# Layer 0 of a two-layer graph network: another order for the first 34 pairs of edge tiles

## The reference, cut to what matters

```python
hid = silu(edge_scalars @ fc_w1 / 8);  w = hid @ fc_w2 / 8          # weights per edge, 224
es, ev = h_s[edge_src], h_v[edge_src]                               # (x @ lin1)[source]
m_s1 = w1 * es * e0;  m_s2 = w4 * dot(ev, e1) / 3
m_v1 = w2 * es * e1;  m_v2 = w3 * ev * e0;  m_v3 = w5 * cross(ev, e1) / 2
agg_s = segment_sum(concat(m_s1, m_s2), edge_dst);  agg_v = segment_sum(...)
o_s = agg_s @ lin2_ws;  o_v = agg_v @ lin2_wv                       # per node
x = layernorm(x + gated(sc + o))
```

## Time and profile before

| | |
|---|---|
| time, median of 3 runs | 2036.88 us (2024.79 to 2044.89) |
| the profiled execution, its own time | 2023.73 us |
| its span in the profile | 2022.0 us, 47808 instructions |
| busy over the span: PE, DVE, ACT, POOL | 1426.0, 1449.6, 1060.1, 1471.5 us |
| chain that ended last, shares | POOL 28%, issue 23%, DMA 16%, DVE 12%, PE 9%, ACT 8% |
| TensorE clock granted, mean | 0.88 |

### The profile page before, as it was taken

The page is one execution under the profiler, slowest core; times in us unless marked ns, Lnnn a source line. Parts: engine busy times, 40 slices in busy tenths (PEclk is TensorE's granted clock), DMA queues, the critical chain, the costliest instruction groups (busy, mean ns, idle before and its releaser), DMA issues.

```text
span 2022.0 us, 47808 instructions
## 1 busy us (share of the span) xinstructions
PE 1426.0 (71%) x10327; PEld 1275.2 (63%) x10327; DVE 1449.6 (72%) x5759; ACT 1060.1 (52%) x3502; POOL 1471.5 (73%) x1923
## 2 busy tenths in 40 slices
PE   6668888888878668888868999988888898100000
PEld 5567777777767557666748988888888888000000
DVE  6448777777767539999975766666666666099998
ACT  3324444444444329999964555555554454056666
POOL 4357878778888548788865777777777777378876
PEclk9779989989999979999988999999999999555555
DMA  9996666666667669999956777777777776499997
GB/s 377 391 281 134 136 131 138 136 133 138 136 131 139 144 183 336 339 338 338 338 181 167 173 174 166 172 165 170 163 173 163 165 170 143 102 362 402 397 391 289
DMA packets 254140, 440.03 MB, mean 218 GB/s; under 512 B 33454, under 2 KB 131408, under 8 KB 250832
## 3 DMA queue, kind: packets, MB, share of 16 engines
q1 hardware_dynamic: 150256, 310.00, 46.0%
q0 software_dynamic: 75264, 67.79, 23.8%
q10 hardware_dynamic: 28512, 61.22, 7.9%
HBM read 235.60 MB, written 203.27 MB: 217 GB/s over the span
## 4 chain that ended last, share of the span: by engine, by line
POOL 28%; issue 23%; DMA 16%; DVE 12%; PE 9%; ACT 8%; ACTq 3%; DVEq 1%; SPq 1%; POOLq 0%
POOL table L553 16%; DMA table<-sums,row_all 11%; POOL xg L529 8%; ACT y L911 6%; DVE stats L1152 4%; DVE res L1113 3%; DMA attrT<-in_attrT 2%; DMA xg<-x_rows,src_all 2%; DVE res L1102 1%; POOL half_rstd L591 1%; ACTq L923 1%; PE ps L700 1%; PE ps L686 1%; PE ps L702 1%; PE ps L650 1%
## 5 line engine op out<-in xcount | busy, mean ns | idle before, releaser
L553 POOL DMA_INDIRECT table<-sums,row_all x392 | 631.1, 1610 | 271.2 <-issue 109.0
L911 ACT ACTIVATE y<-res,norm 128x160 f32<-128x160 f32 x756 | 330.2, 507 | 132.5 <-POOL norm L593 68.3
L847 ACT COPY msg<-ps 128x192 f32<-128x192 f32 (+1 forms) x196 | 57.6, 294 | 537.7 <-PE ps L720 533.1
L529 POOL DMA_INDIRECT xg<-in_x_rows,src_all x196 | 200.0, 1021 | 64.8 <-issue 62.0
L529 POOL DMA_INDIRECT xg<-x_rows,src_all x196 | 195.4, 997 | 64.3 <-issue 58.8
L1062 DVE SCALAR_TENSOR_TENSOR x1g<-ps,a_all,x1g 128x160 f32<-128x160 f32 x392 | 132.4, 379 | 130.3 <-PE ps L741 130.3
L1152 DVE BATCH_NORM_STATS2 stats<-res 128x6 f32<-128x160 f32 x784 | 196.0, 312 | 2.6
L1018 DVE TENSOR_TENSOR pe<-ps,ea_all 128x192 f32<-128x192 f32 x196 | 70.0, 357 | 175.9 <-ACT msg L847 130.0
L700 PE MATMUL ps<-weights,midT 128*128 128x128 f32 (+1 forms) x784 | 164.5, 294 | 20.6 <-DVE msg L1023 19.3
L591 POOL TENSOR_TENSOR half_rstd<-var,minus_half 128x8 f32<-128x8 f32 x98 | 164.4, 1678 | 14.5 <-POOL var L589 0.4
L650 PE MATMUL ps<-ident,xg 128*128 128x128 f32 x392 | 89.3, 311 | 100.1 <-ACT xz L834 94.0
(11 more groups left out here) (122 smaller groups left out, 4546.1 us busy)
## 6 DMA issues: line engine op xcount, KB each, us to landing
tab<-table SPq DMA_DIRECT2D x98, 384.0 KB, 5.0
table<-zeros SPq DMA_DIRECT2D x24, 1536.0 KB, 9.3
table<-zeros SPq DMA_DIRECT2D x98, 324.0 KB
tab<-table SPq DMA_DIRECT2D x98, 324.0 KB, 5.4
xzT<-in_xzT SPq DMA_DIRECT2D x98, 320.0 KB, 4.8
x1g<-x_rows SPq DMA_DIRECT2D x98, 320.0 KB
base_rows<-x1g SPq DMA_DIRECT2D x98, 320.0 KB, 2.5
x1g<-base_rows SPq DMA_DIRECT2D x98, 320.0 KB, 4.9
```

The lines of the kernel that those rows point to most:

```text
L529: pool.indirect_dma_start(out=xg[j % RING][:, t, 0:width], out_offset=None, in_=rows, in_offset=bass.IndirectOffsetOnAxis(ap=src_all[:, at ...
L553: pool.indirect_dma_start(out=table[l], out_offset=bass.IndirectOffsetOnAxis(ap=row_all[:, at:at + 1], axis=0), in_=sums[j % 4][:, t, 0:W] ...
L911: last = nc.scalar.activation(y[u][:, t, :], res[u][:, t, :], ACT.Identity, scale=rstd[u][:, t:t + 1], bias=shift[u][:, t:t + 1])
```

## The change

`run_stages` gets a parameter `ramp`. With it, stage number n of the list, with lag L, of pair j is sorted in the written-out part by (j + L*(pace + (1 - pace)/100), n), where pace is j/ramp and at most 1. With ramp 0 this is the old order. With 24, all stages of pair 0 stand together, and the distance of pair j's stages is j/24 of a step per lag; from pair 24 on it is a whole step as before. The stage named `behind` (PE's `hidden`) is put right behind the stages of lag 1 of the pair before it. The written-out part of PE, ACT and DVE grows from 10 to 34 steps, and the loop has 8 turns of 8 steps in place of 11. For layer 1 the arguments give the old order. POOL's and SP's orders in layer 0 are the old ones.

```diff
-def run_stages(eng, base, count, depth, stages, unroll=4):
+def run_stages(eng, base, count, depth, stages, unroll=4, ramp=0, fixed=(), behind=None):
     assert (count - depth) % unroll == 0
-    for k in range(base, base + depth):
-        for lag, f in stages:
-            if k - lag >= base:
-                f(k - lag, k - lag - base, (k - lag) % unroll)
+    first = []
+    for n, (lag, f) in enumerate(stages):
+        for j in range(depth - lag):
+            pace = 1 if f in fixed or not ramp else min(1, j / ramp)
+            at = (j + lag * (pace + (1 - pace) / 100), n)
+            if f is behind and j > 0 and ramp:
+                pace = min(1, (j - 1) / ramp)
+                at = (j - 1 + pace + (1 - pace) / 100, len(stages) if pace < 1 else n)
+            first.append((*at, j, f))
+    for _, _, j, f in sorted(first, key=lambda w: w[:3]):
+        f(base + j, j, (base + j) % unroll)
...
-                    run_stages(pe, 0, NP, 10, [(1, first_map), (0, hidden), (1, edge_weights), (0, turn_x),
-                                               (3, second_map), (2, turn_mid), (5, sum_pair)], RING)
+                    run_stages(pe, 0, NP, 34, [(1, first_map), (0, hidden), (1, edge_weights), (0, turn_x),
+                                               (3, second_map), (2, turn_mid), (5, sum_pair)], RING, 24, (), hidden)
...
-                    run_stages(act, 0, NP, 10, [(0, copy_z), (1, copy_h), (0, hidden_act), (0, copy_xT),
-                                                (3, copy_message), (2, copy_midT), (5, copy_sums)], RING)
+                    run_stages(act, 0, NP, 34, [(0, copy_z), (1, copy_h), (0, hidden_act), (0, copy_xT),
+                                                (3, copy_message), (2, copy_midT), (5, copy_sums)], RING, 24)
...
-                    run_stages(dve, 0, NP, 10, [
+                    run_stages(dve, 0, NP, 34, [
                         (4, message_vectors), (0, scale_attr), (2, compare), (4, message_sum), (2, mark_later),
-                        (1, products), (2, step_rows), (3, choose_rows)], RING)
+                        (1, products), (2, step_rows), (3, choose_rows)], RING, 24)
```

More of the change, by code:

```diff
@@ L766, in _ @@
                                                 (1, turn1a), (3, second_map), (2, turn_mid), (1, turn1b),
-                                                (2, nodes1b), (5, sum_pair)], RING)
+                                                (2, nodes1b), (5, sum_pair)], RING, 0, (turn1a, turn1b, nodes1a, nodes1b), hidden)
                 def nodes0(g, m, u):
@@ L891, in _ @@
                                                  (1, copy_nTa), (3, copy_message), (2, copy_midT), (0, copy_z1),
-                                                 (1, copy_nTb), (5, copy_sums)], RING)
+                                                 (1, copy_nTb), (5, copy_sums)], RING, 0, (copy_nTa, copy_nTb, copy_z1))
                 def gates(g, m, u):
@@ L1071, in _ @@
                 if l == 0:
-                    run_stages(dve, 0, NP, 10, [
+                    run_stages(dve, 0, NP, 34, [
                         (4, message_vectors), (0, scale_attr), (2, compare), (4, message_sum), (2, mark_later),
-                        (1, products), (2, step_rows), (3, choose_rows)], RING)
+                        (1, products), (2, step_rows), (3, choose_rows)], RING, 24)
                 else:
                     run_stages(dve, NP, NP, 10, [
-                        (4, message_vectors), (2, compare), (4, message_sum), (2, add_self_a), (1, products), (2, add_self_b)], RING)
+                        (4, message_vectors), (2, compare), (4, message_sum), (2, add_self_a), (1, products), (2, add_self_b)], RING, 0, (add_self_a, add_self_b))
                 if l == 0:
```

## The result

The changed kernel takes 2128.36 us (median of 4 runs, 2115.29 to 2134.93) against 2030.84 for the kernel before, measured beside it: ratio 1.0468, 95% interval 1.0408 to 1.0528. It is slower by about 95 us. The direction was as forecast, but the time lies above the range (2045 to 2105), and the forecast loss of 47 us is about half of the measured one.

The account below looks back on a forecast made before the run. POOL was taken to set the pace from pair 8, at 6.6 us a pair. The profiled 2023.7 us plus 47 for the slower start gave 2071, and 13.2 for the median 2084; forecast 2080, range 2045 to 2105.

Parts of the forecast that it names:

- The place: Layer 0's edge stage: its end is set by scatter 13 plus 84 times 6.6 us, as POOL cannot run faster later.
- the slow level of PE: Pairs 0 to 4: PE runs at 1.2 GHz, being busy only 55% of the time in the serial order.
- the clears held: SP's last eight table clears move from 88.84 to 119.7 us to about 130 to 162, costed at nothing.
- the loop's turns without gain: Three fewer loop turns in the edge stage, costed at nothing (between 0 and -12.5 us).
- The latency of a pair: Pairs 0 to 4 do not overlap, so their period is one pair's latency: 17.7 us slow, 12.9 fast.
- pairs 13 to 24: first map, edge weights, products and transposes of mid still form a cycle, 5.9 fast ... 5 more: These stages cycle in 5.9 us, sums come every 6.85 to 7.0 us against 6.6, adding 5 us.
- 14.5 taken: Pairs 5 to 7: only the last stage overlaps; 15.5 us a pair slow, 10.8 fast, 14.5 assumed.
- 11 taken: Pairs 8 to 12: the last two stages overlap; 13.0 us a pair slow, 9.3 fast, 11 assumed, plus 2 for deepening distance.
- PE fast all along: Rival, chance 0.12: PE at its fast level, 12.9 us for pairs 1 to 4; +12 us, median 2049.
- Slower still: Rival, chance 0.03: PE's slow level lasts to pair 24, whose cycle is then 9.8 us; +90, 2127 us.
- The lead is kept: Rival, chance 0.05: a pair passes in at most 12.6 us, scatter 8 comes at 130 instead of 138; -8, 2029 us.
- the turns of the loop count: Rival, chance 0.02: the old loop's waits had delayed scatters, so fewer turns give -12.5, 2024 us.

Follow-up runs that it names:

- the run with PE kept busy: The changed kernel with idle matrix multiplies added on PE in layer 0's early pairs, up to pair 16: 2058.98 us against 2006.89, ratio 1.0248.
- the written-out code: The kernel before, in its old order of stages, with 34 steps of PE, ACT and DVE written out instead of 10: 2025.65 us against 2029.18, ratio 0.9996.
- the seven idle multiplies: The changed kernel with 7 unread matrix multiplies on PE behind the hidden layer of pairs 1 to 8: 2099.76 us, ratio 1.0356.

## Why the prediction was wrong, step by step

**Held.** The place (pairs 1 to 24, through scatters that nothing can speed up later), pairs 0 to 4 serial, the slow level of PE in them, the clears held to 135 to 162 us and load 15 at 173.48 (forecast near 168) at a cost of 1 to 2 us, the loop's turns without gain, POOL's waits for the copy of sums (119.1 us from 39 to 234, forecast some 100). The latency of a pair was put at 17.7 us and is 18.05; for the fast level at 12.9, and the run with PE kept busy has 13.24. That PE would be slow in these pairs was a judgement, and it came true. Scatter 0 was put at 35.5 and came at 39.31 here, but at 34.65 to 35.73 in six experiments whose pair 0 is the same. In the profiled execution ACT was late once; PE's hidden layer, and ACT's copy of h behind it:

```profile
21.07 0.79 PE L665 MATMUL ps<-attrT,weights 128*128 128x128 f32 x2
...
26.12 0.42 ACT L827 COPY hs<-ps 128x320 f32<-128x320 f32 x1 [7.63 <-remote]
```

That is 7.63 us of idle time, some 4 more than at the same place of those six (3.46 to 3.61). What held ACT is not in the trace, and it stays open.

**The step that failed: "pairs 13 to 24: first map, edge weights, products and transposes of mid still form a cycle, 5.9 fast ... 5 more".** It followed PE's order alone. On DVE the message operations of a pair slide behind the products of the pair two later, and that closes a second, longer cycle: second map, first map, edge weights, hidden, copy of h, products, message, second map. From scatter 12 to scatter 24 the loss grew by 31.1 us, not 5. In pairs 17 to 22 alone it is 22.8, and moving the two operations brings most of that back (43.7 us for the six pairs instead of 62.2). Pairs 13 to 16 took 7.9 us each, not the 7.0 of the forecast, and 23 and 24 took 8.0; these 6 us no experiment explains.

**The terms that were too small: "14.5 taken" for pairs 5 to 7 and "11 taken" for 8 to 12.** They took 17.2 and 12.1 us each, 8.1 us more in three pairs and 3.5 in five. The windows of the two stretches (busy PE, PEld, DVE, ACT, POOL; clock, DMA share, GB/s):

```profile
130.00:163.00 33.00, 21.42 (x84) 17.03 (x80) 12.04 (x57) 6.78 (x22) 10.04 (x8) 0.54 0.90 345
163.00:224.00 61.00, 40.25 (x212) 34.88 (x212) 27.27 (x133) 17.14 (x56) 26.77 (x21) 0.72 0.53 136
```

The clock of 0.54 says that PE ran almost wholly at the slow level in pairs 6 and 7, and 0.72 that the next five pairs had the mix that I had assumed. But the level is not the main thing: wholly slow pairs were priced at 15.5, and in the run with PE kept busy, at the fast level, pairs 5 to 7 took 12.9 each instead of 10.8. Scatter 5 came at 129.55, a full 18.0 behind scatter 4: the overlap of the last stage begins a pair later than I had it. Scatter 6 follows at 14.3. Scatter 7 follows at 19.3, and ACT's copies of sums and of h around it show why:

```profile
143.14 0.48 ACT L869 COPY sums<-ps 128x384 f32<-128x384 f32 x1 [1.49 <-PE ps L727]
...
146.13 0.42 ACT L827 COPY hs<-ps 128x320 f32<-128x320 f32 x1 [2.51 <-PE ps L665]
...
160.52 0.43 ACT L827 COPY hs<-ps 128x320 f32<-128x320 f32 x1 [3.45 <-issue]
...
162.40 0.48 ACT L869 COPY sums<-ps 128x384 f32<-128x384 f32 x1 [1.28 <-PE ps L727]
```

From copy of h to copy of h it is 14.4 us, the period that I had forecast. From copy of sums to copy of sums it is 19.3, since PE's sum, which for pair 6 still stood ahead of the next pair's first map (140.88 against 142.89), for pair 7 stands behind that pair's first map, edge weights and hidden (160.24). This step in the order cost 4.9 us, and I had put 2 us for all such steps. With the late start (3.8) and 1.4 in pairs 1 to 4, these terms make 16.9 us at scatter 12 (223.65 against the forecast 206.8). Pairs 13 to 24 add 26 more. 20 of them are in the six pairs of the ring (62.2 us; the forecast's 7.0 a pair makes 42, and with the message moved they take 43.7), and 6 are the ones above.

**The rivals.** "PE fast all along" is what the run with PE kept busy made true up to about 125 us. It was priced at +12 us; that run is 50.5 us late at scatter 97, or 28.5 with the ring gone too: the price lacked the same cycle, and pairs 5 to 12 were too cheap in it (10.8 and 9.3 us priced; 12.9 measured in pairs 5 to 7, and 12.1 in 8 to 12, where PE did not stay fast). "Slower still" gave the right time, +90 and 2127 us, but by luck: it wanted the slow level up to pair 24, while from 255 to 317 us the clock is 0.83 and the place of two operations on DVE makes the pace. "The lead is kept" fails at pair 1 (57.37 against 57.70), and "the turns of the loop count" fails with the written-out code (0.9996). The range was too narrow since its upper end held only the sizes of the terms that I had, and none for a cycle through an engine whose order I had not laid beside the others.

## What to carry to other kernels

When each engine has its own list and runs it in order, a change of distances must be read as a ring over all lists: write down for one pair in the middle of the change what stands ahead of each stage on its engine, and follow it until it closes. The mere latency of one item is what a serial start costs, and it can be dearer than the sum of the fast durations: here PE, idle 7 of 18 us, stood at 1.2 GHz, and a pair took 18.05 us instead of 13.24. An earlier first result is worth nothing where the second one sets the pace: with pair 0 alone run through at once, scatter 0 came 9.7 us earlier and the stage ended 2.7 us later (727.55 for scatter 97).

## What the runs showed of the hardware

In the changed kernel the granted clock column reads 1.00 from 39 to 130 us, with every multiply at the slow duration (0.66 us for a pair of transposes). With the seven idle multiplies it reads 0.60 for 57 to 75 us, where most durations are slow. With PE kept busy it reads 1.00 again for the same stretch, now with the fast durations (0.41). So a reading of 1.00 ahead of the first lower one says nothing about the level in these traces, and the text goes by the durations. And 2.96 us of idle multiplies, placed behind 3 us of work, were followed by about 2 us at the fast level, a gap of 0.94 us among them; with no gap over 1 us the whole pair ran at it.
